# The first layer as another program: shared experts first, 1024 tokens at a time with seven block products, then all typed experts in a row

## The chip, the cores and the metric

The kernel runs on one core of a Trainium2 chip. The metric is the device time of one execution in microseconds; a kernel is timed in several runs and the median is given. TensorE (PE) does the matmuls, and its weight loads are listed apart as PEld. VectorE (DVE), ScalarE (ACT) and GpSimd (POOL) do the elementwise work, and SyncE (SP) issues most of the transfers. Every engine works through its own instructions in order; between engines there are only semaphores.

## What is computed

Four layers, each added to or applied on `x` of 8 x 256 tokens x 256 features, all in fp32. The change touches the first, L0:

```python
def _dense(x, wi, wo):                      # wi 256 x 1024, wo 1024 x 256
    return jax.nn.relu(x @ wi) @ wo
s0, s1, s2 = (_dense(h, share_wi[j], share_wo[j]) for j in range(3))
idx_a, idx_b = type_idx, type_idx + 1       # one type per batch row of 256 tokens
out_a = relu(h @ expert_wi[idx_a]) @ expert_wo[idx_a]
out_b = relu(h @ expert_wi[idx_b]) @ expert_wo[idx_b]
expert_out = out_a * wa + out_b * wb        # wa, wb from softmax(gate_vecs / 0.1)
gi = concatenate([expert_out[:, 0], s0[:, 0], s1[:, 0], s2[:, 0]], axis=-1)
g = softmax(relu(gi @ gate_w1) @ gate_w2)   # four gates per batch row, from its first token
out = expert_out * g0 + s0 * g1 + s1 * g2 + s2 * g3
```

`x = x + L0(x)` is followed by L1 (eight gated experts and a shared one of the same size), L2 (a small adapter with a layer norm) and L3 (a linear map chosen per batch row). These stay as they are.

## The kernel before

Features lie on the 128 partitions in two halves (`DT` = 2), tokens along the free dimension. Each fp32 product is made of three matmuls on a rounded high part and a remainder (`product`: high x high, high x low, low x high, L424 to L426), so weights, inputs and hidden tiles all exist as `hi` (an ACT copy or relu) and `lo` (a subtraction on DVE or POOL).

L0 works in `NB` = 4 blocks of 512 tokens. In each block the list `L0_JOBS` is run: shared expert 0, typed 0, shared 1, typed 1, shared 2, typed 2, typed 3. A job has eight steps, one per 128 hidden features. A step is an up product (`l0_up`, six matmuls into one of four PSUM banks), the relu on ACT (L907), the low part on DVE (L1599), and two steps later the down product (`l0_down`, six matmuls into `sum0` or `sum1`). A shared step works on 512 columns, a typed step on the 256 tokens of a batch row. The twelve weight matrices of the shared experts are loaded once, split once and kept in SBUF (`W`, 96 KB per partition). Typed weights stream through four `raw` buffers in chunks of 512 KB; ACT makes high parts (L874), POOL the low part of the up weights (L1203), DVE that of the down weights (L1622).

`l0_take` moves a finished sum: shared ones to `acc` (L1490), typed ones scaled into `x`. The gate's hidden sum is collected on DVE (`gate_partial`, L1518) and summed over the partitions by small fp32 matmuls (`gate_first`, L513) in step 3 of the next block; `gate_hidden`, `gate_shifted` and `gate_probs` follow in steps 3 to 5, and `mix` adds the parts of the block before to `x` in steps 5, 6 and 16 to 22. The gate of the last block is done in the first steps of L1. Blocks 1 and 2 are one hardware loop.

L1 already uses another scheme. It takes two 512-token blocks and two 128-row weight tiles at a time and replaces eight block products by seven (`block_product`, L552). For that POOL adds and subtracts blocks of `x` (`x_sums`) and of the weights (`weight_sums`), and the results are put together from PSUM banks `A` and `Bk` by ACT copies (L1017) and DVE adds (L1658). Only up products are made so. TensorE's order is written out:

```python
earlier(0); first_products(0); first_products(1); earlier(1)    # earlier(d): down product of the slot before
second_products(0); second_products(1); earlier(2)
third_products(0); third_products(1); earlier(3)
fourth_product(0); fourth_product(1)
```

The weights of L1's first expert are prepared on POOL and ACT in the last L0 block, beside typed and shared steps.

Of the kernel before, what the change touches and what calls it, by code (L numbers as in the profile page):

```python
# [17 lines left out]
B, S, D, F = 8, 256, 256, 1024  # L18
P = 128
# [9 lines left out]
L0_JOBS = [("shared", 0), ("expert", 0), ("shared", 1), ("expert", 1), ("shared", 2), ("expert", 2), ("expert", 3)]  # L29
NJ = len(L0_JOBS)  # L30
L0_STEPS = NJ * FT
L0_ALL = NB * L0_STEPS
EX_STEPS = 4 * FT
EX_CH = EX_STEPS // 2
SUMS = [0, 1, 0, 1, 0, 1, 0]
PLAIN0 = 4 + 4 * NSH
# [28 lines left out]
def job_of_expert(j):  # L65
    return [i for i, (kind, n) in enumerate(L0_JOBS) if kind == "expert" and n == j][0]


def exout_at(k, first, last_block):

    q = (k + 1) // 2
    if k == 0 or (k % 2 == 1) != (q % 4 == 0):
        return None

    if first and q == 5 or last_block and q in (9, EX_CH):
        return None
    return q


def local_step(k):  # L80

    return FT * job_of_expert(k // FT) + k % FT

def stream_table():
    sh = lambda j, m, h: ("plain", 1 + 4 * j + 2 * h + m)
    t = [("plain", 0), sh(0, 0, 0), sh(0, 1, 0), sh(0, 0, 1), sh(0, 1, 1),
         sh(1, 0, 0), sh(1, 1, 0), sh(1, 0, 1), ("expert", 0), ("expert", 1), ("expert", 2), ("expert", 3), ("expert", 4), ("expert", 5),
         sh(1, 1, 1)] + [sh(2, m, h) for h in range(2) for m in range(2)]  # L90
    t += [("plain", 13), ("plain", 14), ("plain", 15)]
    t += [("expert", q) for q in range(6, 58)]
    t += [("plain", PLAIN0 + r) for r in range(3)]
    t += [("expert", q) for q in range(58, 64)]
    t += [("plain", PLAIN0 + r) for r in range(3, L1_CH * NE1 + B)]
    return t
# [6 lines left out]
def build(nc, xT_d, sh_d, ex_d, l1_d, types_d, types_row_d, gvec_d, gw1_d, gw2_d, prob_d, sgate_d, w1_d, w2_d, b1_d, cols_d, w3_d, bias_d, ident_d, out_d):  # L103
# [45 lines left out]
    gpart = place("gate_partial", [P, 2, D], f32)  # L149
# [19 lines left out]
    cg = place("gate_tile", [P, 3, BLK], f32, over="weights", skip=88 * K1)  # L169
    hi = place("hidden_hi", [P, 4, BLK], f32r, over="hidden")  # L170
# [29 lines left out]
    with ctx:  # L200
# [13 lines left out]
        first_hi, first_lo = sem("first_hi"), sem("first_lo")  # L214
        const_full, gw1_full = sem("const_full"), sem("gw1_full")
# [45 lines left out]
        def gate_ps(tb):  # L261

            return sums[0 if isinstance(tb, int) and tb == NB else 1]
# [42 lines left out]
        def raw_fill(key):  # L306

            return 16 * (AT[key] // RAW + 1)
# [1666 lines left out]
```

## Time and profile before

| | |
|---|---|
| median of 3 runs | 1604.03 us (1602.68 to 1605.13) |
| the profiled execution | 1604.2 us, span 1602.4 us |
| instructions | 22577 |
| TensorE busy | 1592.0 us (99%), 7986 matmuls |
| weight loads busy | 1354.9 us (85%) |
| DVE, ACT, POOL busy | 1096.3 (68%), 864.8 (54%), 510.3 (32%) |
| moved by DMA | 79.05 MB, mean 49 GB/s |

Busy shares tell which engine to look at. Matmuls are pipelined, so that the listed duration of one (0.39 us for 512 columns) is longer than the distance between two starts; the distance is what counts. The list of instructions in order of time gives the start, the duration and, in brackets, how long the engine sat idle before it and what ended that. A list of one line's instructions gives the shortest, median and longest duration in ns. A table of stretches gives each engine's busy time in it, TensorE's granted clock as a share of full speed, and the transfers.

### The profile page before, as it was taken

To read this page: it belongs to the slowest core of one execution; us is meant where nothing else is said; L and a number is where in the kernel's file an instruction comes from. 1 tells how busy PE (TensorE), PEld (TensorE's weight loads), DVE (VectorE), ACT (ScalarE), POOL (GpSimd) and SP (SyncE) were. 2 spreads that over 40 slices of the span, in tenths; PEclk is the share of its full clock that TensorE was granted. 3 is DMA by queue.
4 is the path that set the end of the run, shared out by engine and by line. 5 is a ranking of instruction groups with operands and counts; after the bars stand their busy time and mean duration, and the time that the engine had idled before them with its cause. 6 is when DMAs were issued, how large, how long until landed. Compare 5 with 4: busy or idle time off the path is not lost.

```text
span 1602.4 us, 22577 instructions
## 1 busy us (share of the span) xinstructions
PE 1592.0 (99%) x7986; PEld 1354.9 (85%) x7986; DVE 1096.3 (68%) x1661; ACT 864.8 (54%) x1563; POOL 510.3 (32%) x452
## 2 busy tenths in 40 slices
PE   9999999999999999999999999999999999999998
PEld 8898898898897888888888888888888888888888
DVE  6665565466679777777777777776776776656555
ACT  5543343343565665665565565565565565555343
POOL 2121121124745431431431431431431441146110
PEclk9999999999999999999999999999999999999999
DMA  6522131131321010010010010010010000021000
GB/s 226 183 92 68 53 106 52 52 105 53 105 80 40 14 40 27 14 40 27 14 40 27 14 39 27 17 37 27 21 33 27 25 29 27 27 65 44 13 14 27
DMA packets 28763, 79.05 MB, mean 49 GB/s; under 512 B 4838, under 2 KB 9830, under 8 KB 28534
## 3 DMA queue, kind: packets, MB, share of 16 engines
q1 hardware_dynamic: 28070, 76.39, 14.8%
q8 instruction: 58, 0.95, 0.2%
q0 software_dynamic: 304, 1.10, 0.2%
q14 instruction: 43, 0.35, 0.1%
q10 hardware_dynamic: 288, 0.26, 0.1%
HBM read 75.64 MB, written 2.10 MB: 49 GB/s over the span
## 4 chain that ended last, share of the span: by engine, by line
PE 98%; DVE 1%; DMA 0%; issue 0%; ACT 0%; SPq 0%; DVEq 0%
PE sum L424 13%; PE sum L425 13%; PE sum L426 13%; PE up L556 13%; PE up L558 13%; PE up L557 13%; PE up L424 7%; PE up L425 6%; PE up L426 6%; DMA raw<-in_shared 0%; PE sum L738 0%; PE sum L513 0%; PE sum L704 0%; PE sum L764 0%; PE sum L763 0%
## 5 line engine op out<-in xcount | busy, mean ns | idle before, releaser
L1028 ACT ACTIVATE hidden_hi<-up_tile 128x512 fp32r<-128x512 f32 x256 | 161.2, 630 | 187.3 <-DVE up_tile L1663 163.3
L907 ACT ACTIVATE hidden<-up 128x256 fp32r<-128x256 f32 (+1 forms) x224 | 106.3, 475 | 247.0 <-PE sum L426 203.7
L1658 DVE TENSOR_TENSOR gate_tile<-up,gate_tile 128x512 f32<-128x512 f32 x192 | 130.0, 687 | 142.3 <-PE up L558 142.3
L1668 DVE TENSOR_TENSOR hidden_lo<-up_tile,hidden_hi 128x512 fp32r<-128x512 f32 x256 | 196.0, 785 | 44.0 <-ACT hidden_hi L1028 44.0
L1599 DVE SCALAR_TENSOR_TENSOR hidden<-up,hidden 128x256 fp32r<-128x256 f32 (+1 forms) x224 | 120.3, 537 | 154.4 <-ACT hidden L907 153.1
L556 PE MATMUL up<-x_sums,gate_up 128*128 128x512 f32 x512 | 199.5, 390 | 0.0
L426 PE MATMUL sum<-hidden_hi,down 128*128 128x512 f32 x512 | 199.4, 390 | 0.0
L424 PE MATMUL sum<-hidden_hi,down 128*128 128x512 f32 x512 | 199.4, 390 | 0.0
L425 PE MATMUL sum<-hidden_lo,down 128*128 128x512 f32 x512 | 199.4, 389 | 0.0
L558 PE MATMUL up<-x_sums,gate_up 128*128 128x512 f32 x512 | 199.4, 389 | 0.0
L557 PE MATMUL up<-x_sums,gate_up 128*128 128x512 f32 x512 | 199.4, 389 | 0.0
L1663 DVE TENSOR_TENSOR up_tile<-up_tile,gate_tile 128x512 f32<-128x512 f32 x192 | 183.2, 980 | 2.2
L1203 POOL TENSOR_TENSOR expert_in<-raw,expert_in 128x512 fp32r<-128x512 f32 x64 | 83.2, 1300 | 318.1 <-ACT expert_in L874 318.1
L1021 ACT ACTIVATE gate_tile<-gate_tile 128x512 f32<-128x512 f32 x192 | 119.8, 633 | 90.4 <-DVE gate_tile L1658 88.2
L556 PE MATMUL up<-x_hi,gate_up 128*128 128x512 f32 x384 | 149.9, 390 | 0.8 <-DVE up_tile L1663 0.8
L557 PE MATMUL up<-x_lo,gate_up 128*128 128x512 f32 x384 | 149.6, 390 | 0.0
L558 PE MATMUL up<-x_hi,gate_up 128*128 128x512 f32 x384 | 149.6, 390 | 0.0
L1017 ACT ACTIVATE gate_tile<-up 128x512 f32<-128x512 f32 x192 | 110.5, 594 | 72.0 <-PE up L558 65.6
L1203 POOL TENSOR_TENSOR gate_up<-raw,gate_up 128x384 fp32r<-128x384 f32 x64 | 72.3, 1130 | 204.3 <-ACT gate_up L971 204.3
L1658 DVE TENSOR_TENSOR up_tile<-up,up_tile 128x512 f32<-128x512 f32 x192 | 130.2, 687 | 1.9
L1017 ACT ACTIVATE up_tile<-up 128x512 f32<-128x512 f32 x192 | 112.0, 600 | 21.2 <-PE up L558 15.6
L424 PEld LDWEIGHTS sum<-hidden_hi,down 128*128 128x128 f32 x512 | 96.1, 188 | 20.7 <-DVE hidden_lo L1668 0.9
(267 smaller groups left out, 3700.6 us busy)
## 6 DMA issues: line engine op xcount, KB each, us to landing
raw<-in_experts SPq DMA_DIRECT2D x64, 512.0 KB, 3.6
raw<-in_l SPq DMA_DIRECT2D x54, 512.0 KB, 3.5
raw<-in_shared SPq DMA_DIRECT2D x11, 512.0 KB, 5.0
raw<-in_w SPq DMA_DIRECT2D x8, 256.0 KB, 2.5
raw<-in_xT SPq DMA_DIRECT2D x3, 512.0 KB, 5.7
out<-out_stage SPq DMA_DIRECT2D x6, 256.0 KB, 2.1
gate_w<-in_gw POOLq DMA_DIRECT2D x1, 1024.0 KB, 7.8
raw<-in_w SPq DMA_DIRECT2D x16, 64.0 KB, 2.4
```

What stands on the lines that cost most here:

```text
L424: pe.matmul(out, wh, vh, start=start, stop=False)
L425: pe.matmul(out, wh, vl, start=False, stop=False)
L426: return pe.matmul(out, wl, vh, start=False, stop=stop)
L556: pe.matmul(out, wh, vh, start=first, stop=False, skip_group_check=True)
L557: pe.matmul(out, wh, vl, start=False, stop=False, skip_group_check=True)
L558: return pe.matmul(out, wl, vh, start=False, stop=True, skip_group_check=True)
L1017: A(out, ps, ACT.Copy).then_inc(q_done[m], 1)
L1028: A(hi[:, i], cu[:, i], ACT.Copy).then_inc(hi_done, 1)
L1203: return nc.gpsimd.tensor_tensor(dst, src, hi.bitcast(f32), ALU.subtract)
L1658: V.tensor_tensor(t, ps, t, ALU.add).then_inc(c_done[m], 1)
L1663: V.tensor_tensor(cu[:, i], up, cg[:, RING[i]], ALU.mult).then_inc(gat_done, 1)
L1668: V.tensor_tensor(lo[:, i], cu[:, i], hi[:, i].bitcast(f32), ALU.subtract).then_inc(lo_done, 1)
```

## The change

L0 becomes two programs in a row.

**Shared experts.** 24 slots: two halves of 1024 tokens, three experts, four weight pairs. A slot makes the up products of one pair for 1024 tokens with seven block products (`shared_up`, 21 matmuls of 512 columns) and the down products of the slot before (`shared_down`, 4 x 6). Slot 0 makes its four tiles directly, with 24 matmuls, as long as no sums exist. Weights are no longer kept: 24 chunks stream in for the first half and again for the second, and are summed and split each time. ACT copies the first contributions out of PSUM, DVE adds, ACT makes relu and high part, DVE the low part. `x` is now loaded straight into its tile. The shared sums of all four blocks are stored in separate places (`accs`).

**Typed experts.** Four blocks of 32 steps of 256 columns, written out, with no loop. The gate's shared part is made once for all batch rows on TensorE (`gate_shared`); `gate_partial` goes. Mixing is split: `mix_start` on DVE in steps 5 and 6, the scaling of two shared sums on ACT in steps 7 to 10, six additions on POOL (`x_add`), the last shared sum on DVE in steps 20 and 21 (`mix_end`). The preparation of L1's first weights is spread over typed blocks 0 and 1 from three chunks staged apart (`stage`), and that of its x sums over block 3. The last block is mixed in L1 as before.

```diff
-L0_JOBS = [("shared", 0), ("expert", 0), ("shared", 1), ("expert", 1), ("shared", 2), ("expert", 2), ("expert", 3)]
+NJ = 4
+NA = 2 * NSH * 4
 ...
+            sp.dma_start(x[:, 0, 0:BLK], xT_d[:, 0, 0:BLK]).then_inc(first_x, 16)
+            sp.dma_start(x[:, 1, 0:BLK], xT_d[:, 1, 0:BLK]).then_inc(x_in[0], 16)
+            load_x(1)
+            sp.dma_start(raw[:, 0, FIRST[2]], sh_d[0][:, FIRST[2]]).then_inc(raw_full[0], 16)
+            load_chunk(("first", 0), sh_d[1])
 ...
+                    load_chunk(("expert", EX_CH * tb + q), ex_d[t[q // 4] * 4 + q % 4])
+                    if tb == 0 and q == 1:
+                        sp.wait_ge(sh_b[1], 3 * 12)
+                        for r in range(STAGED):
+                            sp.dma_start(stage[:, r], l1_d[r]).then_inc(stage_full[r], 16)
 ...
 TensorE:
+            def shared_slot(a):
+                if a == 0:
+                    shared_first_tiles()
+                    return
+                shared_up(a, "first")          # waits for the low parts of its weight pair (w_lo)
+                shared_down(a - 1, 0)
+                if a > 1:
+                    shared_up(a - 1, "fourth")
+                shared_down(a - 1, 1)
+                shared_up(a, "second")         # waits for x sums 1 to 3, ACT's first copy, DVE's first add
+                shared_down(a - 1, 2)
+                shared_down(a - 1, 3)
+                shared_up(a, "third")
 ...
+                    if tb and n == 3:
+                        if tb == 1:
+                            gate_shared()
                         gate_first(tb)
 ...
 ACT, from slot 0's last tiles on:
+            for i in range(2):
+                shared_x_hi(0, i)
+            act.wait_ge(sh_sum, 4)
+            A(agu[0][:, 0, 1, 3 * P:7 * P], aws[0][:, 1, 3 * P:7 * P], ACT.Copy).then_inc(w_hi, 1)
+            for i in range(2, 4):
+                shared_x_hi(0, i)
+            first_part(adn[1][:, 0].rearrange("p f n -> p (f n)"), raw[:, 1, 512:1024])
 ...
 ACT, at the end of shared_slot(a), behind sh_copied(a, 2), sh_copied(a, 1):
+                if a == 1:
+                    shared_up_hi(1)
+                    shared_down_hi(1)
+                elif a % 2 == 0 and a + 2 < NA:
+                    shared_up_hi(a // 2 + 1)
+                elif a % 2 == 1 and a + 1 < NA:
+                    shared_down_hi((a + 1) // 2)
+                if a in (2, 3):
+                    x_in_hi(a)
 ...
 POOL:
+            shared_x_sum(0, 0)
+            shared_x_sum(0, 1)
+            shared_sums(0)
+            shared_x_sum(0, 2)
+            shared_up_lo(0)
+            shared_x_sum(0, 3)
+            for p in range(1, NAP):
+                shared_sums(p)
+                shared_up_lo(p)
+                shared_down_lo(p)
+                if p == 1:
+                    for i in range(4):
+                        shared_x_sum(1, i)
+                if p in (3, 4):
+                    for i in range(2):
+                        shared_x_lo(1, 2 * (p - 3) + i)
 ...
+            for q in range(NB * EX_CH):
+                expert_lo(q)
+                if q in AFTER:                 # early_sum, early_up_lo, early_down_lo, x_add, x_sum, ...
+                    AFTER[q]()
 ...
 DVE, shared_slot(a): adds and low tiles, then
+                if a in (2, 3):
+                    x_in_lo(a)
+                if a % 4 == 0 and a < NA:
+                    gr, j, _ = shared_of(a - 1)
+                    shared_take(gr, j, 0)
+                    shared_take(gr, j, 1)
 ...
 DVE, l0_block(tb), step n:
+                    if tb and n in (5, 6):
+                        mix_start(tb, n - 5)
+                    if tb and n in (20, 21):
+                        mix_end(tb, n - 20)
 ...
 ACT, l0_block(tb), step n:
+                    if tb and 7 <= n <= 10:
+                        scaled_shared(tb, (n - 7) // 2, (n - 7) % 2)   # waits for both mix_start
```

## Rows read from the trace of the kernel before

**Rows 1.** The page: busy time per engine, and the chain that ended last by engine.

```profile
PE 1592.0 (99%) x7986; PEld 1354.9 (85%) x7986; DVE 1096.3 (68%) x1661; ACT 864.8 (54%) x1563; POOL 510.3 (32%) x452
...
PE 98%; DVE 1%; DMA 0%; issue 0%; ACT 0%; SPq 0%; DVEq 0%
```

**Rows 2.** List in order of time, TensorE, shared steps: start, duration, instruction.

```profile
194.62 0.39 PE L424 MATMUL sum<-hidden,weights 128*128 128x512 f32 x1
...
205.96 0.39 PE L426 MATMUL sum<-hidden,weights 128*128 128x512 f32 x1
```

**Rows 3.** List in order of time, TensorE, typed steps in a row.

```profile
447.00 0.28 PE L424 MATMUL up<-x_hi,expert_in 128*128 128x256 f32 x1
...
449.76 0.28 PE L426 MATMUL sum<-hidden,expert_out 128*128 128x256 f32 x1
```

**Rows 4.** List in order of time at the start; then a piece of the chain there.

```profile
6.83 0.63 ACT L942 ACTIVATE weights<-raw 128x512 fp32r<-128x512 f32 x1 [0.23 <-DMA raw<-in_shared]
...
12.43 0.40 PE L424 MATMUL up<-x_hi,weights 128*128 128x512 f32 x1
...
2.13 6.35 DMA raw<-in_shared
```

**Rows 5.** List in order of time, POOL (380 to 497) and ACT (420): preparing L1.

```profile
380.40 1.75 POOL L1236 TENSOR_TENSOR x_sum_tiles<-x 128x512 f32<-128x512 f32 x1
...
386.44 5.94 POOL L1203 TENSOR_TENSOR x_sums<-x_sum_tiles,x_sums 128x512 fp32r<-128x512 f32 x4
...
419.51 0.79 POOL L1262 TENSOR_TENSOR weight_sums<-raw 128x256 f32<-128x256 f32 x1
...
422.93 1.02 POOL L1203 TENSOR_TENSOR gate_up<-raw,gate_up 128x384 fp32r<-128x384 f32 x1
...
475.30 1.01 POOL L1203 TENSOR_TENSOR gate_up<-raw,gate_up 128x384 fp32r<-128x384 f32 x1
...
480.20 1.02 POOL L1203 TENSOR_TENSOR gate_up<-raw,gate_up 128x384 fp32r<-128x384 f32 x1
...
496.85 2.56 POOL L1203 TENSOR_TENSOR down<-raw,down 128x512 fp32r<-128x512 f32 x2 [11.23 <-ACT down L980]
...
420.30 0.84 ACT L970 ACTIVATE gate_up<-raw 128x768 fp32r<-128x768 f32 x1
421.04 1.05 ACT L971 ACTIVATE gate_up<-weight_sums 128x1024 fp32r<-128x1024 f32 x1
```

**Rows 6.** One line's instructions, DVE: shortest, median and longest ns; SBUF inputs, then PSUM.

```profile
L1663 DVE TENSOR_TENSOR up_tile<-up_tile,gate_tile x192: 676/693/1786, 462.5 to 1411.9; 128x512 f32<-128x512 f32 x192
L1663 DVE TENSOR_TENSOR up_tile<-up,gate_tile x64: 676/691/692, 469.7 to 1413.4; 128x512 f32<-128x512 f32 x64
```

**Rows 7.** TensorE near the end; a stretch (length, busy per engine, granted clock, DMA).

```profile
1571.04 0.30 PE L424 MATMUL up<-x_hi,l_w 128*64 128x256 f32 x1 [2.39 <-DVE x_lo L1788]
1572.06 0.41 PE L425 MATMUL up<-x_lo,last_gate_up 128*128 128x256 f32 x1
1572.27 0.41 PE L426 MATMUL up<-x_hi,last_gate_up 128*128 128x256 f32 x1
...
1572.00:1574.00 2.00, 2.00 (x12) 2.00 (x11) 0.84 (x2) 0.85 (x3) 0.00 (x0) 0.50 0.00 0
```

**Rows 8.** Stretch of typed steps in a row: length, PE, PEld, DVE, ACT, POOL busy, clock.

```profile
433.00:457.50 24.50, 24.50 (x193) 23.90 (x192) 19.35 (x31) 12.63 (x29) 14.32 (x13) 1.00 0.46 151
```

**Rows 9.** The gate's small matmuls in the chain; two blocks, one looped, one unrolled.

```profile
127.49 0.79 PE sum L513 x8
...
127.20:240.47 113.27, 113.27 (x684) 101.27 (x683) 64.76 (x115) 43.95 (x90) 23.25 (x17) 1.00 0.24 75
...
353.70:466.60 112.90, 112.90 (x684) 101.27 (x683) 75.16 (x118) 54.38 (x106) 57.68 (x49) 1.00 0.26 85
```

**Rows 10.** POOL's queue: its configuration records and its first tensor instruction.

```profile
L1203 POOLq MODIFY_POOL_CONFIG  x2: 37/37/37, 9.0 to 9.1; - x2
...
24.79 1.28 POOL L1203 TENSOR_TENSOR expert_in<-raw,expert_in 128x512 fp32r<-128x512 f32 x1 [15.77 <-ACT expert_in L874]
```

More of the change, by code:

```diff
@@ L62, with gu_at, dn_at @@
 STAGES += ["split", "beta", "scaled", "base", "final"]
[L65 to L82, printed above, removed]
-def stream_table():
[L87 to L96, printed above, removed]
+def gu_at(p):
+    return max(2 * p - 1, 0)
+def dn_at(p):
+    return 2 * p
+def stream_table():
+    t = [("plain", 0), ("first", 0)] + [("plain", o) for o in range(1, PLAIN0)]
+    t += [("expert", q) for q in range(NB * EX_CH)]
+    return t + [("plain", PLAIN0 + r) for r in range(STAGED, L1_CH * NE1 + B)]
 STREAM = stream_table()
@@ L261, in gate_ps @@
         def gate_ps(tb):
-            return sums[0 if isinstance(tb, int) and tb == NB else 1]
+            return sums[0]
         def ex_slot(n):
@@ new lines, in shared_down @@
+            def shared_down(a, d):
+                g, j, s = shared_of(a)
+                f, to = TILES[d]
+                pe.wait_ge(sh_lo[d], a + 1)
+                if a < 2:
+                    pe.wait_ge(first_lo, 8 + a)
+                elif a % 2 == 0:
+                    pe.wait_ge(w_lo, dn_at(a // 2) + 1)
+                if s == 0 and d < 2 and a:
+                    pe.wait_ge(sh_taken, 2 * (3 * g + j) - 1 + to)
+                for m in range(DT):
+                    c = slice(m * P, (m + 1) * P)
+                    last = product(sums[1 - to][:, m, :], adn[a % 4][:, 0, f, c], adn[a % 4][:, 1, f, c], hi[:, d], alo[:, d],
+                                   s == 0 and d < 2, s == 3 and d >= 2)
+                last.then_inc(sh_down[d], 1)
@@ L481, in l0_down @@
                 if f == 0:
-                    before = [i for i in range(jj) if SUMS[i] == SUMS[jj]]
-                    if before:
-                        pe.wait_ge(sum_taken, NJ * tb + before[-1] + 1)
-                    elif not first:
-                        back = [i for i in range(NJ) if SUMS[i] == SUMS[jj]][-1]
-                        pe.wait_ge(sum_taken, NJ * tb - NJ + back + 1)
-                    if jj == 1 and not first:
-                        pe.wait_ge(gate_shift, tb)
-                c = slice(0, BLK) if job[0] == "shared" else ex_slot(n)
@@ L812, in scaled_part @@
                     last.then_inc(scaled_done, 1)
-            l0_block(0, first=True)
-            with pe.Fori(1, NB - 1) as tb:
+            for a in range(NA):
+                shared_slot(a)
+            for tb in range(NB):
                 l0_block(tb)
-            l0_block(NB - 1)
             for e in range(NS):
```

1016 lines of the change are left out of this document (635 added, 381 removed).

## The prediction

> **What bounds the kernel now.** I read the page first: TensorE is busy 99% of the span at full clock, and 98% of the chain that ended last is TensorE [rows 1]. A busy share does not say how dense the stream is, so the next view is the instruction list: a matmul over 512 columns starts every 0.2267 us (51 starts from 194.62 to 205.96, [rows 2]), one over 256 columns every 0.120 us (24 starts from 447.00 to 449.76, [rows 3]), and inside layer 0 hardly anything interrupts them. So the kernel costs its matmuls, plus what it loses at the start, at the gates and at the end. All other engines have room on average (DVE 68%, ACT 54%, POOL 32%); what counts is where one of them is late for a matmul. The sum is made against the profiled execution, 1604.2 us, 0.2 above the median of 1604.03.
>
> **Matmuls removed.** Shared experts before: 4 blocks x 24 steps x 12 = 1152 matmuls of 512 columns. After: 24 slots x (21 up + 24 down) = 1080, and 3 more, because slot 0 makes its four tiles directly (24 instead of 21): 1083. Only the up half of a shared expert becomes cheaper, 7/8 of it. 69 x 0.2267 = **-15.6 us**. The typed experts keep their 1536 matmuls of 256 columns. L1 keeps its own.
>
> **Small things on TensorE.** The gate's share of the shared experts moves from DVE to TensorE: 12 small fp32 matmuls, once. Four such take 0.79 us before [rows 9]; **+2.4**. The four per block remain. The loop over blocks is written out: the unrolled block is 112.90 us against 113.27 of a looped one [rows 9], so 2 x 0.35; with DVE's gate_partial gone from the front of L1 (a 0.8 us wait is near it, I give it 0.4), **-1.1**.
>
> **The start.** This is the disputed term, since the new program needs much more preparation before its second pair of slots. Before, TensorE's 25th matmul of the work starts at 12.43 [rows 4]: 24 x 0.2267 = 5.4, so 7.0 us lie outside the work. After, I follow the queues.
>
> - x block 1 (512 KB) now comes ahead of the last 256 KB weight part. Before, that part is used at 6.83, and the 512 KB chunk after it has landed at 8.48 [rows 4], 1.65 us for 512 KB; so block 1 lands at about 7.7, and tiles 2 and 3 of slot 0 start at 9.7 (two ACT copies, DVE's low parts). TensorE then has slot 1's first products and half of slot 0's down products, to 16.5.
> - POOL makes everything slot 1 still lacks, in one queue: two x sums (4 take 6.04, [rows 5]), four half-size weight sums (2.2, half the size of those that take 3.42), a third x sum, a low part (1.3), the fourth x sum: 18.2. ACT stands in its queue at the copy of that fourth sum, and only behind it (and one down copy) makes slot 1's first copy, which the second products wait for: **20.1**, TensorE idle 3.6 us.
> - Slot 2's first products need pair 1's low parts. POOL: sums 3.4 to 21.5; ACT is not free before 23 to 23.5 (its three copies of slot 1) and splits pair 1 (0.84 and 1.05, [rows 5]); POOL's four low parts take 4.90 [rows 5]: **30.4**. TensorE has been out of work since 26 to 27.4.
> - Then POOL: down low parts 2.5, four x sums of the second half 6.0 to 6.8, sums of pair 2 3.4: 42.6. ACT waits for them in slot 2's queue (pair 2), and behind them copies x block 2 (1.05); DVE waits for this copy (x_in_lo, 1.2) at the end of slot 2, ahead of slot 3's first add. So slot 2's fourth product, which TensorE could start at 43.4 to 45, starts at **47 to 48**, and the down product behind it at about 50.
> - At that point 126 matmuls are done, 28.6 us of work: 21.5 us outside the work against 7.0. The start costs **+14.5**. POOL's serial work alone, with never a wait for ACT, gives 8.5 (lower bound); with every DVE instruction held and three clock drops it is 17.
>
> The half clock is in this: before, after an idle TensorE of 2.39 us the granted clock is 0.50 (the 1.2 GHz level) for at least 2 us, in which 256-column matmuls come every 0.21 us [rows 7]; each such drop costs 1 to 1.6 us of work, partly hidden in the next wait. The Trainium skill (TensorE: Matmul & The Clock Gate, "Why this matters for your kernels") likewise advises against idle gaps between bursts; by that rule the change pays beyond its three gaps, and the trace agrees with 2.39 us idle and 0.50 granted.
>
> From slot 4 on the pipeline holds. A slot is 45 x 0.2267 = 10.2 us. DVE has seven instructions of 0.7 (3 adds, 4 low tiles), ACT seven of 0.6 and 1.9 of weights, POOL 11 to 12 us per pair of slots, 20.4. Each tile is ready 0.7 to 2 us before its down product even if DVE is held once: a DVE instruction with both inputs in SBUF takes 0.69 us alone and up to 1.79 beside POOL, one that reads PSUM 0.69 always [rows 6]. The two takes (1.2 each) end just as the next slot's adds are due. I cost the steady slots at nothing; without this cover it would be some 0.5 us per slot.
>
> **From shared to typed.** SP issues the three staged L1 chunks (1.5 MB) ahead of expert chunks 2 and 3, so chunk 2 lands near 8 us into the first typed slot, when it is due; DVE takes two sums and makes the first low parts between them. **+1.5** (0 to 3).
>
> **All typed experts in a row.** A typed step is 12 x 0.120 = 1.44 us. From 433 to 457.5, where typed steps run in a row already, TensorE is busy all 24.5 us and ACT 12.6 of them [rows 8]. New is that the gate and the mixing of a block now lie in typed steps 3 to 10, not in shared steps of 2.72. DVE in steps 5 and 6: three small ones, two mix_start (0.75), a low part of weights (0.69) and two hidden tiles (0.42) are 3.2 against 2.88, more if held; ACT's scaling waits for both mix_start ahead of its next relu. I follow it step by step to a wait of 0.9 us per block (0.5 without holding, 2.3 with all of it), three blocks: **+2.7** (1.5 to 7). POOL has 1.30 per two steps plus one added instruction (1.3 to 1.75) against 2.88, on 35 of the 64 chunks: on the edge, costed at nothing.
>
> One page bears on POOL's first instruction. In the trace of before, POOL's configuration records stand at 9.0 us, and the first tensor instruction only waits for ACT much later, so nothing shows a loading time [rows 10]. The Trainium skill (GPSIMD Engine Reference, "2.1 Instruction dispatch") says that the first call to a freshly loaded kernel pays a load of about 6 us that no instruction shows. By that, POOL's first x sum would start near 10 and not 7.7, and as ACT has slack there the start would cost about 1.3 us more, an estimate from this page; the trace does not decide, and the sum does not use it.
>
> **Sum.** -15.6 + 2.4 - 1.1 + 14.5 + 1.5 + 2.7 = +4.4; 1604.2 + 4.4 - 0.2 = **1608.5 us** (forecast, chance 0.42, its own range 1605 to 1613).
>
> **Rivals.**
> 1. The start costs only POOL's serial work, and neither the crossing nor the typed blocks wait: -15.6 + 2.4 - 1.1 + 8.5 = -5.8, **1598.2 us**, faster. The point that decides: ACT free at the moment the pair 1 sums are ready, and slot 2's fourth product by 43.5. For it: waits I add can overlap. Against it: ACT's queue order. Chance 0.18.
> 2. The start as worked out, but the typed run has no wait: -15.6 + 2.4 - 1.1 + 14.5 = +0.2, **1604.2 us**, no change. For it: at 433 to 457.5 DVE worked 19.35 of 24.5 us and TensorE never waited. Chance 0.22.
> 3. POOL does not keep up with the typed run: 1.30 + 1.75 held is 3.05, with a delay by DVE on both 3.2, against 2.88, so 0.2 to 0.3 late on each of 35 chunks once its lead of about 1.2 us is used: some 8 us more than the forecast, **1617 us**. For it: POOL's durations in the trace reach 1.75; against it: most are 1.30. Chance 0.18.
>
> **Numbers.** Range 1598 to 1617. A measurement of this kernel can tell about 0.2% (3.2 us) from no change: below 1600.8 is faster, above 1607.2 slower. Faster: most of rival 1 and a tail of rival 2, 0.20. Same: most of rival 2 and the lower part of the forecast, 0.29. Slower: the rest of the forecast and rival 3, 0.51.
>
> **What would show it.** In the profile after: 69 fewer 512-column matmuls at the same 0.227 us spacing; TensorE idle near 17 to 20, 26 to 30 and 44 to 47, each ended by ACT copies or POOL low parts, with granted clock 0.5 behind them; the first typed matmul at about 261 us; small waits on DVE and ACT in steps 5 to 9 of typed blocks 1 to 3; L1's first product some 4.5 us later than before. I am wrong if the stalls of the first 50 us sum to under 12 us, if the steady slots are longer than 10.3 us, or if typed blocks are longer than 32 x 1.44 = 46.1 us plus 2 to 3 us.

## The result and the profile after

The changed kernel takes **1621.78 us** (median of 4, 1620.72 to 1623.1) against 1604.58 for the kernel before in the same comparison (4 runs, 1602.68 to 1605.26): ratio **1.0107** (95%: 1.0095 to 1.0119), 17.2 us slower. The forecast of 1608.5 us has the right sign; the size is wrong, and the time lies above the range of 1598 to 1617. All times of stretches below are from the profiled execution, 1622.5 us with a span of 1620.7.

The page after, first busy times, then the granted clock in 40 slices and the chain that ended last by engine; they answer to [rows 1]:

```profile
PE 1591.2 (98%) x7941; PEld 1351.8 (83%) x7941; DVE 1132.7 (70%) x1661; ACT 938.3 (58%) x1696; POOL 682.8 (42%) x600
...
PEclk8999999999999999999999999999999999999999
...
PE 93%; DVE 3%; ACT 1%; POOL 1%; issue 1%; DMA 0%; SPq 0%; ACTq 0%; DVEq 0%
```

TensorE is as busy as before, though it has 15.6 us less to do: at half clock matmuls of 512 columns start every 0.43 us instead of every 0.2267, and all of that time counts as busy. What tells is the chain, from 98% TensorE to 93%, and the view of waits (what TensorE waited for, us in total, times, longest):

```profile
PE sum L438 <- DVE expert_out L2004: 5.2, 7, 1.7
PE up L438 <- DVE x_lo L1840: 4.1, 1, 4.1
PE up L446 <- POOL shared_up L1429: 3.3, 1, 3.3
PE up L446 <- ACT gate_tile L998: 3.1, 1, 3.1
...
PE sum L625 <- DVE gate_products L1950: 1.9, 1, 1.9
...
PE sum L438 <- DVE shared_lo L1845: 1.1, 1, 1.1
```

Two groups: four waits of the first 55 us (x_lo, shared_up, gate_tile, shared_lo), and the low parts of the typed down weights (`expert_out`) with the gate, all behind 265 us. The sums of waits are smaller than the loss, so I kept books by time: from a mark to a mark, less the matmuls between at 0.2267 and 0.120 us.

| stretch | time | work | outside the work | in the kernel before | loss |
|---|---|---|---|---|---|
| to the first typed matmul | 265.5 | 239.4 (1056 matmuls) | 26.1 | 7.0 (to 12.43) | +19.1 |
| from there to L1's first product | 211.2 | 189.0 | 22.2 | 6.1 | +16.1 |
| work of L0 | | | | | -15.6 |
| L1's first product to the end | 1144.0 | | | 1145.3 | -1.3 |

The sum is 18.3 us, the two profiled executions differ by 18.3. The forecast had +14.5 for the first row and, gates, crossing, mixing and loop together, +5.5 for the second: the start is 4.6 us over it, the typed run 10.6. The steady slots are as forecast: from 55 to 270 us TensorE is busy 215.0 of 215 us.

**The start.** The chain, then the list in order of time (brackets: idle before, and what ended it):

```profile
1.70 8.08 DMA x<-in_xT
...
10.47 2.95 DVE x_lo L1840 x2
```

```profile
13.46 0.80 PE L438 MATMUL up<-x_hi,shared_up 128*128 128x512 f32 x1 [4.14 <-DVE x_lo L1840]
...
18.99 0.60 ACT L1003 ACTIVATE hidden_hi<-up 128x512 fp32r<-128x512 f32 x1 [1.96 <-PE up L440]
...
21.22 1.44 POOL L1429 TENSOR_TENSOR shared_up<-shared_sums_up,shared_up 128x512 fp32r<-128x512 f32 x1 [4.70 <-ACT shared_up L1076]
...
26.14 0.77 PE L446 MATMUL up<-shared_x_sums,shared_up 128*128 128x512 f32 x1 [3.05 <-ACT gate_tile L998]
...
36.57 0.77 PE L446 MATMUL up<-x_hi,shared_up 128*128 128x512 f32 x1 [3.26 <-POOL shared_up L1429]
...
54.60 0.50 PE L438 MATMUL sum<-hidden_hi,shared_down 128*128 128x512 f32 x1 [1.09 <-DVE shared_lo L1845]
```

The four gaps are those of the forecast (9.7, 20.1, 30.4, about 50), 3.8 to 6.2 us later. The lines to look at are the second and the third: POOL, which I took to work without a pause, stands 4.70 us waiting for ACT's copy of the weight sums, and ACT stands ahead of it at slot 0's last tile, which TensorE had only just made.

**The typed run.** One line's instructions (shortest, median, longest ns), the low parts of the typed down weights, in the kernel before and in the changed one:

```profile
L1622 DVE TENSOR_TENSOR expert_out<-raw,expert_out x64: 678/693/1373, 25.3 to 456.1; 128x512 fp32r<-128x512 f32 x64
```

```profile
L2004 DVE TENSOR_TENSOR expert_out<-raw,expert_out x64: 674/1204/1848, 273.4 to 475.6; 128x512 fp32r<-128x512 f32 x64
```

Two stretches of the changed kernel (length, busy of PE, PEld, DVE, ACT, POOL, granted clock, DMA), around the gate of block 1:

```profile
323.00:328.00 5.00, 5.00 (x39) 5.00 (x37) 1.73 (x3) 0.90 (x2) 1.94 (x2) 0.80 0.52 185
328.00:333.00 5.00, 5.00 (x25) 5.00 (x25) 2.40 (x10) 1.34 (x4) 0.00 (x0) 0.51 0.09 19
```

And the list in order of time at the gate of the last block:

```profile
429.80 1.29 POOL L1429 TENSOR_TENSOR expert_in<-raw,expert_in 128x512 fp32r<-128x512 f32 x1
431.05 1.26 POOL L1429 TENSOR_TENSOR x_sums<-x_sum_tiles,x_sums 128x512 fp32r<-128x512 f32 x1
...
429.90 2.43 DVE L1947 TENSOR_SCALAR gate_products<-gate_w,gate_hidden 128x4 f32<-128x4 f32 x2
...
432.78 0.39 PE L625 MATMUL sum<-gate_products,ones 128*128 128x8 f32 x2 [1.93 <-DVE gate_products L1950]
```

The median low part takes 1.20 us where it took 0.69, since POOL now works beside typed steps far more. The 12 small matmuls of the shared gate (from 323.64) and the block's own gate take 4.5 us. The clock falls during them, near 326, without an idle gap ahead of it, and half clock lasts for another 4.6 us behind them. And two instructions of four columns take 1.21 and 1.31 us, 2.43 together, beside two POOL instructions of 1.3.

By block, from the first typed matmul over the three gates (326.4, 378.3, 428.4) to L1: 60.9, 51.8, 50.1 and 48.4 us, of which outside the products 4.4 (2.8 of it the shared gate), 5.8, 4.0 and 8.0. A block's own gate, two sets of small matmuls, is about 1.2 of each of the last three.

### The profile page after: what moved, and what is told of

The parts are those of the page before. It is cut to its first block, busy times and chain, and to the rows that moved or that the text cites. A ratio compares the mean times of both kernels' runs of the same rounds, so it can differ in the third digit from the quotient of the medians.

```text
span 1620.7 us, 22419 instructions
## 1 busy us (share of the span) xinstructions
PE 1591.2 (98%) x7941; PEld 1351.8 (83%) x7941; DVE 1132.7 (70%) x1661; ACT 938.3 (58%) x1696; POOL 682.8 (42%) x600
## 4 chain that ended last, share of the span: by engine, by line
PE 93%; DVE 3%; ACT 1%; POOL 1%; issue 1%; DMA 0%; SPq 0%; ACTq 0%; DVEq 0%
PE up L670 13%; PE up L672 12%; PE up L671 12%; PE sum L438 12%; PE sum L440 12%; PE sum L439 12%; PE up L438 4%; PE up L439 3%; PE up L440 3%; PE up L446 2%; PE up L448 2%; PE up L447 2%; DVE expert_out L2004 1%; DMA x<-in_xT 0%; DVE x L1987 0%
## 5 line engine op out<-in xcount | busy, mean ns | idle before, releaser
L1429 POOL TENSOR_TENSOR gate_up<-raw,gate_up 128x384 fp32r<-128x384 f32 x60 | 68.0, 1133 | 204.2 <-ACT gate_up L1198 204.2
L1243 ACT ACTIVATE up_tile<-up 128x512 f32<-128x512 f32 x192 | 112.1, 600 | 21.3 <-PE up L672 15.6
L1556 POOL TENSOR_TENSOR weight_sums<-raw 128x256 f32<-128x256 f32 x30 | 28.9, 963 | 204.7 <-PE up L672 204.7
L670 PEld LDWEIGHTS up<-x_sums,gate_up 128*128 128x128 f32 x512 | 96.1, 188 | 20.2 <-ACT gate_tile L1243 0.2
## 6 DMA issues: line engine op xcount, KB each, us to landing
x<-in_xT SPq DMA_DIRECT2D x3, 512.0 KB, 10.2
```

Source lines behind the costliest of these rows:

```text
L670: pe.matmul(out, wh, vh, start=first, stop=False, skip_group_check=True)
L1243: A(out, ps, ACT.Copy).then_inc(q_done[m], 1)
L1429: return nc.gpsimd.tensor_tensor(dst, src, hi.bitcast(f32), ALU.subtract)
```

## The experiments

Every profile is read at the same marks: first typed matmul, the gates of blocks 2 and 3, L1's first product, the span (us).

| kernel | first typed | gate 2 | gate 3 | L1 | span | outside the work to first typed |
|---|---|---|---|---|---|---|
| before | | | | 457.08 | 1602.4 | |
| changed | 265.54 | 378.25 | 428.36 | 476.72 | 1620.7 | 26.1 |
| s1_order | 261.06 | 374.21 | 424.32 | 472.65 | 1616.4 | 21.7 |
| s2_loads | 263.86 | 376.83 | 426.95 | 475.33 | 1619.2 | 24.5 |
| s3_queue | 261.00 | 373.76 | 423.89 | 471.47 | 1616.9 | 21.6 |
| t1_gate | 266.58 | 378.06 | 428.17 | 475.78 | 1621.2 | 27.2 |
| t2_adds | 263.33 | 376.77 | 425.57 | 473.71 | 1619.1 | 23.9 |
| t3_lows | 263.25 | 377.68 | 427.81 | 474.56 | 1618.5 | 23.9 |
| d1_direct | 255.15 | 366.62 | 416.75 | 465.94 | 1609.9 | 15.1 |
| d2_direct_gate | 255.62 | 366.75 | 416.86 | 463.60 | 1609.0 | 15.5 |
| d3_start | 250.97 | 361.93 | 412.06 | 460.41 | 1604.5 | 10.9 |
| d4_all | 249.78 | 361.72 | 410.59 | 457.60 | 1603.0 | 9.7 |
| d5_all | 249.56 | 363.54 | 412.42 | 457.72 | 1603.1 | 9.5 |
| d6_all | 250.32 | 362.32 | 411.22 | 456.50 | 1600.3 | 10.2 |

(From d1_direct on there are 1059 matmuls up to the first typed one, 240.1 us.) When x block 1 has landed shows in POOL's first instruction, which waits for nothing else. The changed kernel and t1 to t3 have the same start and give 263.3 to 266.6, with that landing at 8.4 to 9.9: a first typed matmul is good to 3 us from one profile. From POOL's first instruction to the first typed matmul these four take 254.8 to 257.0 us, s1_order 252.0, s2_loads 255.8, s3_queue 251.4; this takes the landing out of the comparison. From gate 2 to gate 3 all nine profiles with the original mixing there give 50.11 to 50.13.

### s1_order: the queue of ACT at the start

```diff
-tiles 1, 3 of slot 0; x sums 0, 1; weight sums of slot 1; x sums 2, 3      # ACT; DVE's low parts alike
+x sums 0, 1; weight sums of slot 1; tile 1; x sum 2; tile 3; x sum 3
```

> Against the changed kernel; ScalarE (ACT) copies the x sums 0 and 1 and slot 1's weight sums ahead of slot 0's tiles 1 and 3, DVE's low parts follow the same order. Theory A, order of ACT's queue: in the changed kernel POOL stands from 16.5 to 21.2 us waiting for ACT's copy of the weight sums, which stands behind the copy of slot 0's last tile (TensorE, 19.0). Then POOL's low part moves from 21.2 to about 16.5, slot 1's second products from 26.1 to about 21, slot 2's first products from 36.6 to 31 to 32, the first typed matmul from 265.5 to 260 to 261: 4.5 to 5.5 us less. Theory B, the preparation as such is too long (POOL's serial work and the half clock behind each gap): what the first gap gives back is lost in the next, first typed matmul at 264 or later, under 1.5 us less.

First typed matmul at 261.06, 4.5 us earlier, kernel 1618.3 us (one run). POOL's low part no longer waits:

```profile
14.50 0.63 ACT L1073 ACTIVATE shared_up<-shared_sums_up 128x512 fp32r<-128x512 f32 x1 [1.44 <-POOL shared_sums_up L1468]
...
15.66 1.73 POOL L1428 TENSOR_TENSOR shared_up<-shared_sums_up,shared_up 128x512 fp32r<-128x512 f32 x1
...
23.83 0.50 PE L446 MATMUL up<-shared_x_sums,shared_up 128*128 128x512 f32 x1 [0.56 <-DVE gate_tile L1848]
```

Theory A, though slot 1's second products start at 23.8 and not at the expected 21. About 1 us of the 4.5 is x block 1, which landed earlier here (copied at 8.96); counted from POOL's first instruction, 2.8 to 5.0 us are won. It is an order, not an amount of work, that made POOL late.

### s2_loads: the loads behind x block 1

```diff
+            sp.wait_ge(x_in[1], 16)
             load_chunk(("first", 0), sh_d[1])      # and all later loads
```

> Against the changed kernel; the loads behind the first weight parts (a down chunk, two weight chunks, x blocks 2 and 3) are issued only once x block 1 has landed. Theory A, the transfers share the engines: x block 1 lands at 7.7 to 8.3 instead of 9.8, tiles 2 and 3 of slot 0 start at 11.5 to 12 instead of 13.5, and the first typed matmul is 1.5 to 2 us earlier (if slot 1's weight chunk, now landing later, is not what is late next; then 0). Theory B, x block 1 waits only for the bytes issued before it: it lands at 9.8 again, and the kernel is 0 to 2 us slower, since down chunk and pair 1 land some 4 us later.

ACT's copy of x block 1 starts at 7.96 instead of 9.81, TensorE's tiles at 11.63 instead of 13.46, the first typed matmul 1.7 us earlier; kernel 1621.1 us (one run). The time alone shows nothing: t2_adds and t3_lows, whose start is that of the changed kernel, reach the first typed matmul at 263.3, earlier than the 263.86 here. The landing does: in the three profiles in which the chunks wait for x block 1 (this, d5_all, d6_all) POOL's first instruction starts at 8.07 to 8.09, in the ten others at 8.4 to 9.9. So transfers issued later can delay it; my 7.7 for the landing had counted only the bytes ahead. The gap behind x block 1 is not its landing alone, though: DVE's two low parts, 1.3 us in the forecast, took 2.95 beside POOL's sums.

### s3_queue: x blocks 2 and 3, and the second half's x sums

```diff
+                if a in (2, 3): x_in_hi(a)          # ACT: ahead of shared_up_hi, shared_down_hi
-                if p == 1: 4 x shared_x_sum(1, i)   # POOL
+                if p == 2: 4 x shared_x_sum(1, i)
```

> Against the changed kernel; ACT copies x blocks 2 and 3 ahead of the weights of pairs 2 and 3, and POOL makes the four x sums of the second half behind pair 2's low parts instead of ahead of pair 2's sums. Theory A: DVE's low part of x block 2 (50.65 us) is what slot 2's fourth product waits for, so it moves to about 46, the half clock and the 1.1 us wait at 54.6 go, and the first typed matmul is 3 to 4 us earlier. Theory B: the wait only moves to slot 4's first products (pair 2's low parts) or to slot 3's tiles, under 1 us is won.

First typed matmul 4.5 us earlier (3.4 to 5.6 counted from POOL's first instruction), kernel 1618.8 us (one run). The fourth product's wait is gone. Part of it comes back, as theory B said, once:

```profile
70.46 0.50 PE L438 MATMUL sum<-hidden_hi,shared_down 128*128 128x512 f32 x1 [1.66 <-DVE shared_lo L1845]
```

### t1_gate: the small matmuls one by one

```diff
-                        if tb == 1: gate_shared()        # 12 fp32 matmuls in a row, step 3
+                    if spread[0]: gate_shared()          # one behind every third matmul, steps 3 to 5
```

> Against the changed kernel; the 12 small fp32 matmuls of the gate's shared part stand one by one behind every third matmul of typed steps 3 to 5 of block 1 instead of in a row, the block's own gate follows two steps later. Theory A: in a row they cost 2.9 us plus a drop of the granted clock to half (328 to 333 us, about 2.4 us); spread, the drop goes: no half clock there, block 1 about 2 to 2.5 us shorter. Theory B: the drop comes from something else, or small matmuls between others cost more each (their weight load is not hidden): block 1 equally long or longer by up to 3 us.

The half clock is gone (1.00 granted from 320 to 370 us, 0.93 in the changed kernel), but from the first typed matmul to gate 2 only 1.2 us are won (111.5 against 112.7), not 2 to 2.5. d1_direct shows why. There the 12 matmuls stand in a row as in the changed kernel, yet no half clock followed; instead the waits appear which the slow matmuls had covered, 0.23, 0.26, 0.33 and 0.75 us from 324 to 332, and the same stretch takes 111.5 us too. So the half clock costs 1.2 us net against this profile of the changed kernel, and spreading the matmuls wins nothing over an execution without it: the slow stretch gave DVE time. The 1.2 is not a fixed price: other executions with the drop take 112.8 to 114.4, but d3_start, with its 12 matmuls in a row and 0.50 granted from 313.7 to 317.1, takes only 111.0.

### t2_adds: POOL's additions of the mixing

```diff
-G(x[:, dt, sl], x[:, dt, sl], other, ALU.add)
+G(x[:, dt, sl][:, 0:1], x[:, dt, sl][:, 0:1], other[:, 0:1], ALU.add)
```

> Against the changed kernel; POOL's 18 additions of the mixing (three typed blocks, six each) work on one column instead of 512, so the mixed x is wrong. Theory A, in the typed run DVE's low parts with both inputs in SBUF are held by POOL's instructions and so come late for the down products: without the additions the waits at steps 10 to 20 of blocks 1 to 3 go (343.7, 349.7, 394.1, 400, 446.8, 452.7, 458.8 us), first typed matmul to L1's first product 2 to 3 us shorter. Theory B, DVE's own number of instructions makes them late: under 0.5 us.

The kernel leaves out 511 of the 512 columns of each addition.

```profile
L2004 DVE TENSOR_TENSOR expert_out<-raw,expert_out x64: 673/694/1781, 271.2 to 472.6; 128x512 fp32r<-128x512 f32 x64
```

The median low part falls from 1.20 to 0.69 us without a change on DVE. From gate 2 to gate 3 it takes 48.80 instead of 50.11: 1.3 us, and the wait of 0.75 in step 12 is gone. Two waits of 0.28 and 0.33 us in steps 8 and 9 stay. Over the whole typed run 0.8 us are won, not the 2 to 3 expected: the stretch to gate 2 was 0.7 longer here, the last block only 0.2 shorter. But in this execution the last block has a drop of the clock (0.51 granted from 430.5 to 434) that the changed kernel's profile has not, so its time is no clean reading. TensorE's waits in blocks 1 to 3 fall from 7.1 to 4.8 us. Theory A in the mechanism; the size in time is shown by block 2 alone, 1.3 us.

### t3_lows: L1's x sums in the last block

```diff
-for i, at in enumerate((3, 4, 11, 12)):      # chunk of the last block behind which POOL makes low part i
+11: low part 0; 12: low part 1; 13: low parts 2 and 3
```

> Against the changed kernel; in the last typed block POOL makes the first two low parts of L1's x sums behind chunks 11 and 12 instead of 3 and 4 (the other two behind 13). Theory A: DVE's gate products (four instructions of 4 columns), of which the first two took 2.43 us beside POOL instead of 0.36 in block 1, are held by these low parts, and the wait of 1.93 us at 432.8 goes, as does part of the 1.7 at 440: 2 to 3 us less. Theory B: they are late for another reason (ACT, the sums' take), nothing changes; or the low parts, now close to the end of the block, are late for L1 and give 1 us back.

The gate products' wait falls from 1.93 to 0.84 us, that of 1.68 at 440 us to 0.34; gate 3 to L1's first product takes 46.8 instead of 48.4. 1.6 us, under the expected 2 to 3. The stretch to gate 2, which the edit doesn't touch, was 1.7 longer in this execution, so that the typed run as a whole shows nothing (211.3): only the local reading decides. The first of the two gate products still takes 1.21 us, beside POOL's expert low part, which was not moved; the second, beside which the moved low part had stood, falls from 1.31 to 0.22. So instructions of four columns were held by POOL.

### d1_direct and d2_direct_gate: slot 1 without sums

```diff
+T0(0) T0(2) T1(0) T1(2)                      # TensorE: tiles of slots 0 and 1, first 512 tokens
+T0(1) down(0,0) T0(3) down(0,2) T1(1) down(0,1) T1(3) down(0,3) down(1,0) down(1,2) up(2,"first")
-shared_sums(0); shared_up_lo(0)              # POOL
```

> Against the changed kernel; slot 1 is made directly as slot 0 (24 matmuls instead of 21, no sums of x or of its weights needed), TensorE makes its two tiles of the first 512 tokens while x block 1 is under way, POOL goes straight to the x sums and pair 1; later loads wait for x block 1, and ACT copies x blocks 2 and 3 ahead of weights. Theory A, the start is lost to preparation that pair 0 needs: with 27 matmuls' worth of tiles more in hand, TensorE waits only for x block 1 (about 14 us, 24 matmuls done), slot 2 follows at about 30, pair 1 being ready at 25 to 27; first typed matmul at 249.5 to 252, so 14 to 16 us less, kernel 1606 to 1608. Theory B, POOL's preparation (x sums 6.2, pair 1 8.6 plus ACT's copies, pair 2) is what limits the first 50 us in any order: slot 2 or slot 4 waits, first typed matmul at 257 or later, 1612 or more.

> The start of the run before, the spread gate of block 1 and the moved low parts of block 3 together. If the three are independent: 15 + 2 + 2.5 us less than the changed kernel, 1602 to 1604, that is equal to the kernel before. If the start only moves the preparation's lateness on: 1608 or more.

The diff shows a part: loads behind the down chunk also wait for x block 1, slot 0's last weight part is issued ahead of it, ACT copies x blocks 2 and 3 ahead of weights as in s3_queue, and the tiles of both slots have new places in the queues of ACT and DVE.

d1_direct: 1611.7 us (one run), first typed matmul at 255.15, so 15.1 us outside the work instead of 26.1, for three matmuls more. How much of the 11.0 us comes from making slot 1 directly was not separated: no run has the changed orders of s1_order, s2_loads and s3_queue together without it, and s1_order and s3_queue alone won 4.5 each. x block 1 leaves 1.0 us of idle time, slot 2's first products start at 27.44 with 0.35. That fits theory A, but is 3 to 6 us short of its number, and one wait accounts for most of them:

```profile
39.18 0.84 ACT L1047 ACTIVATE shared_up<-raw 128x768 fp32r<-128x768 f32 x1 [5.79 <-POOL shared_sums_up L1511]
...
42.64 0.79 PE L439 MATMUL sum<-hidden_hi,shared_down 128*128 128x512 f32 x1 [3.91 <-DVE shared_lo L1883]
```

ACT stands 5.79 us at a copy for slot 4, and slot 2's tile, which TensorE needs now, is behind it. d2_direct_gate: 1610.76 us (5 runs), 1.0039 (1.0025 to 1.0053) of the kernel before, outside its expected 1602 to 1604, with the same stall; the typed run won 2.8 us (208.0 against 210.8).

### d3_start and d4_all: that stall, and the rest of the typed run

```diff
-p == 1: x sums of the second half            # POOL, ahead of pair 2's sums
+p == 2, ahead of shared_down_lo(2)
-a == 2: constants()                          # DVE; now a == 5
-mix_start in steps 5, 6                      # d4_all alone: 5, 7 (ACT's scaling 8 to 11)
```

> Slot 1 made directly, as before; in addition POOL makes the four x sums of the second half behind pair 2's first low parts (not ahead of pair 2's sums), and DVE's constants and ACT's exponentials of the type gates stand two to three slots later. Theory A, what is left of the start in d1_direct is one stall: ACT stood 5.8 us at the copy of pair 2's sums (39.2 us), with slot 2's tile behind it in its queue, TensorE idle 3.9 us at 42.6 and at half clock after it. Then pair 2's sums are ready at 33.5, the stall goes, and the first typed matmul moves from 255.2 to 249 to 250.5; kernel 1605.5 to 1607. Theory B, POOL's total work up to slot 4 is the limit and the stall comes back elsewhere (slot 4's first products, the low parts of the second half's sums, the take behind slot 4, as at 70.5 us in s3_queue): 253 or later.

> The same start; the spread gate, the moved low parts of the last block, and mix_start in steps 5 and 7 instead of 5 and 6 (ACT's scaling one step later). Block 2 of the typed run, from gate to gate, has taken 50.11 us in every run but the one without POOL's additions (48.80). Theory A, DVE's pile-up in steps 5 to 8 costs the two small waits (0.28 and 0.33 us) there: block 2 takes 49.3 to 49.6; first typed matmul to L1's first product 206 to 207.5 (211.2 in the changed kernel); kernel 1602 to 1604, just faster than the kernel before or equal. Theory B, the waits of a block are those of its additions and takes alone: block 2 stays at 50.1, kernel 1604 or more.

d3_start: 1607.38 us (10 runs), ratio 1.0018 (1.0008 to 1.0027). First typed matmul at 250.97, 4.2 us earlier, 0.5 later than theory A's bound, and the kernel 0.4 above its 1607. The stall is gone, and nothing came back but 0.41 us at 60.4. The constants and exponentials moved in the same run; that the order of POOL's sums is the cause rests on the wait, which ended with those sums. It would be some 1.5 us more with the same first 10 us: here the first matmuls ran at half clock (every 0.43 us until 9.8), ACT stood at slot 0's tiles and copied x block 1, landed at 9.5, only at 11.2; in d1_direct it did so at 9.6. Of the start's loss of 19.1 us against the kernel before, 3.9 are left (10.9 against 7.0), and 0.7 of work for three matmuls.

d4_all: 1606.11 us (11 runs), 1.0008 (0.9999 to 1.0017). From gate 2 to gate 3 48.87 us instead of 50.11 to 50.13: theory A, with more than the expected 0.5 to 0.8, as much as t2_adds won by leaving the additions out: either end of the pile-up can be relieved. The typed run takes 207.8 us (expected 206 to 207.5), and the kernel's time is 2 us above the expected; the list shows two waits for POOL, the larger in block 1 (2.3), this one in the last block:

```profile
451.78 0.36 PE L439 MATMUL up<-x_hi,expert_in 128*128 128x256 f32 x1 [1.28 <-POOL expert_in L1482]
```

### d5_all and d6_all

```diff
 d5: the down chunk too waits for x block 1; x sum low part 3 behind chunk 15; mix_end in steps 19, 21
 d6: block 1 alone: additions from chunk 6 (not 5), mix_start in 7, 8, mix_end in 22, 23
```

> As d4_all, and: the down chunk too is loaded only once x block 1 has landed (it landed at 9.6 and 11.2 us in the last two profiles, and the kernel's own runs spread by 4 us); of L1's x sum low parts in the last block two no longer stand behind one chunk of POOL (there TensorE waited 1.28 us for POOL's expert low part at 451.8); mix_end stands in steps 19 and 21 instead of 20 and 21 (waits of 0.28 and 0.69 us at 443 and 445). Theory A, each of these waits is a matter of what stands together in a queue: x block 1 lands at 8.0 to 8.8 in every run, first typed matmul at 248.5 to 249.5, last block (gate to L1's first product) 45 to 45.6 instead of 47.0; kernel 1602.5 to 1604.5 with a spread under 2.5 us. Theory B, the engines' load in these steps is full and the waits only move: last block 46.5 or more, kernel 1605.5 to 1606.5 again.

> As d5_all, with the queue order of block 1 alone changed: its mixing starts two steps later than in the other blocks (its gate does), so POOL's additions now begin one chunk later (they stood waiting for DVE 3.5 us, with the expert low part behind them for which TensorE waited 2.3 us at 326.9), and DVE's mix_end stands in steps 22 and 23 instead of 19 and 21 (there DVE waited for POOL's last addition and TensorE 1.55 us at 343.8). Theory A: both waits go, block 1 (gate to gate) takes 47.2 to 48 instead of 49.65, L1's first product 455.5 to 456.5 in a profile with the same start, kernel 1602 to 1604, faster than the kernel before by 0.05 to 0.2%. Theory B, POOL with 1.30 and 1.75 us per chunk is itself at TensorE's pace of 2.9 us in these steps, so the waits only come later: block 1 at 49 or more, kernel 1605.

d5_all: 1605.05 us (11 runs), 1.0000 (0.9991 to 1.0009), spread 2.7 us (d4_all 4.0); expected were 1602.5 to 1604.5 and under 2.5. Both local parts of theory A are there: x block 1 landed at 8.1 (in d6_all too; 9.2 to 9.7 in d1 to d4), and the last block takes 45.3 us. But ACT copies x block 1 only at 9.8, behind slot 0's second tile, so the start wins nothing; and time came back in block 1, 49.65 us instead of 48.08 between its gate and gate 2:

```profile
326.91 0.36 PE L439 MATMUL up<-x_hi,expert_in 128*128 128x256 f32 x1 [2.30 <-POOL expert_in L1482]
343.79 0.36 PE L439 MATMUL sum<-hidden,expert_out 128*128 128x256 f32 x1 [1.55 <-DVE expert_out L2063]
```

d6_all mends these two by order alone: block 1 takes 47.90, L1's first product is at 456.50, and the kernel takes **1602.39 us** (11 runs, 1600.77 to 1603.57) against 1605.13 (15 runs): 0.9986 (0.9977 to 0.9995). It is the only version faster than both kernels, by 0.14% against the kernel before, which is less than the 0.2% of the forecast's scale. In its profile block 1 still waits 1.54 us for one low part.

Not all of this gain lies in layer 0. In the profiles d6_all reaches L1's first product 1.2 us before d5_all and 0.6 before the kernel before; the other 1.5 us against either are the stretch behind it, where d5_all and the kernel before have a drop of the clock (0.96 granted from 1560 to 1600) and d6_all has none (1.00). The mean granted clock is 1.000 in 7 of the 11 runs of d6_all and in 1 of the 15 of the kernel before; whether the new order has to do with that is open. In layer 0 the 15.6 us of matmuls saved are all but used up: the start costs 3.2 us more than before and three matmuls 0.7, the typed run 11.1.

## Why the forecast was wrong

**Matmuls, -15.6.** Right, at the same spacing; L1 is untouched.

**gate_shared, +2.4.** 2.8 (323.64 to 326.42). What I had not foreseen is the half clock behind it, 1.2 us net in this profile (t1_gate, d1_direct), in d3_start nothing.

**Start, +14.5.** It cost 19.1. The gaps, their place and their cause were named rightly, their times were 3.8 us late at the first one and 4.6 to 6.2 at the others. The first error is a term: landing at 7.7 (it was 9.8 in the profile, 8.0 with the chunks behind it held back), and 1.3 us for DVE's two low parts that took 2.95 beside POOL, although [rows 6] gave the held duration, which I had used in the typed run and not here. The second is a step left out: I had POOL work through, and did not put slot 0's tiles 1 and 3 into ACT's queue ahead of the weight sums (s1_order, up to 4.5 us). Nor do POOL's terms up to 18.2 add up: from 7.7 they give 17.2, and the last sum gives 1608.4 us. Half clock was in the sum with 1 to 1.6 us for each of three drops; about 32 matmuls came every 0.43 us or more (12, 6 and 14 behind the three gaps), some 6.5 us gross. How much of that another wait would have cost was not measured. The upper bound of 17 assumed every hold and three drops and was still too low, since it took the landing for certain.

**Steady slots, 0.** Right.

**Crossing, +1.5.** A wait of 0.27 us and a few slow starts, about 1 us in all. Right.

**Typed blocks' mixing, +2.7.** This is the step that failed most. Beyond the gates the changed kernel loses 1.6 us in block 0 (the crossing is in it), about 1 in block 1 (the half clock covers the rest), 2.7 in block 2 and 6.8 in the last. With the gates, the crossing and the half clock taken out of the +16.1, 9 to 11 us are left for this term (an estimate from the books). The prediction's own sign of being wrong is met: blocks 1 and 2 take 51.8 and 50.1 us, over 46.1 plus 2 to 3. I had followed DVE's queue with 0.69 us for the low part and held values as an extra; the held value is the rule there (median 1.20). And I had looked at the mixing alone: the last block also carries the x sums for L1, which in the kernel before lay beside shared steps of twice the length, and these met the gate's small instructions (1.9 and 1.7 us, t3_lows). The last block alone all but reaches the bound of 7 for three.

**Loop and gate_partial, -1.1.** Not taken apart by any run.

**The rivals.** Rival 1 (start costs POOL's serial work) is refuted by ACT's queue, but d3_start shows that its kind of number can be had with slot 1 made directly and other orders: 10.9 us outside the work, 3.9 more than before where this rival had 8.5. Rival 2, a typed run without a wait, rested on the stretch of 24.5 us in [rows 8]; that stretch has no gate and no mixing in it. Rival 3 gave 1617 us and was nearest, by the wrong mechanism: in the changed kernel's profile no typed step waited for POOL itself; it made DVE late. POOL's own lateness exists: in block 0, which these runs share with the changed kernel, TensorE waited 0.25 to 0.77 us for it in s3_queue, t1_gate, t2_adds and t3_lows, and up to 2.3 us later on (d4_all, d5_all), where it had stood waiting for DVE or had two extra instructions behind one chunk.

**The page on POOL's first instruction.** The traces decide most of it now. In s2_loads POOL's configuration records stand at 4.2 us and its first tensor instruction starts at 8.07, 0.11 behind ACT's copy of the same x block: 3.9 us, and those were spent waiting for the transfer. The Trainium skill (GPSIMD Engine Reference, "2.1 Instruction dispatch") gives about 6 us for such a load; one that began at 4.2 would have ended at 10.2, and no such time is seen here. A load of under 3.9 us could be hidden in the wait.

## What to carry to other kernels

Saved matmuls pay only when what prepares them has room, and at the start of this kernel it had none. Doing the second unit plainly too (three more matmuls, 0.7 us), together with other orders of loads and of ACT's queue, bought 11 us; how much of that the orders alone would buy was not measured, so try them first. To forecast such a start, write down each engine's queue in full, and ask of each instruction that waits what is queued behind it; a copy for slot 4 ahead of a tile for slot 2 cost 4 us, and order alone took the typed run from 211.2 to 206.2 us. What the new layout costs there stays: 17.2 us outside the work in d6_all against 6.1 before. When elementwise work is moved from long steps to short ones, take the durations held by the other engine as the normal case.

## What the hardware showed

**DVE and POOL.** Instructions of DVE that read only SBUF are held for the length of POOL's: 0.69 us becomes 1.20 in the median and 1.85 at most, and a TENSOR_SCALAR of four columns took 1.2 us instead of 0.23. The relu with one input in PSUM took 404 to 427 ns in all 128 cases. The Trainium skill (SBUF — State Buffer, "SBUF: two separate sides") describes the pair of ports that the two share as an exclusive lock, which goes to whichever starts first and for its whole instruction. The traces agree: the short instructions of DVE ran about as long as POOL's beside them (1.21 and 1.31 us beside 1.29 and 1.26). I had read [rows 6] as a matter of large tiles.

**The granted clock** of the changed kernel fell to half in the course of small fp32 matmuls (in s3_queue and d3_start 0.5 and 1.2 us behind them), during which TensorE is listed as busy throughout (5.00 of 5.00 us, 323 to 328), with no idle gap; a clock that only idle time brings down, which I had assumed, is not what this trace shows. It fell in seven of the eight profiles with the 12 in a row (not in d1_direct) and in none of the five with them spread. Behind the small matmuls it stayed down for 4.6 us in the changed kernel and in t3_lows, 3.4 in s3_queue. What a drop costs differs: the last block of the changed kernel's order takes 48.3 to 48.4 us in four profiles without one, 47.6 in s3_queue and t1_gate and 49.2 in d1_direct with one, since the slow matmuls cover waits.

**Transfers.** The 512 KB of x block 1, issued at 1.70 us, landed between 8.4 and 9.9 with the same program (by POOL's first instruction), and at 8.0 with the chunks behind them held back (s2_loads). Even that is 6.3 us, while the median of the typed chunks of the same size is 3.3; the transfers issued ahead of it are the likely reason, which no run tested.

**The end.** From L1's first product to the end, profiles with the same instructions fall into two groups: 1143.8 to 1144.1 us in seven without a drop of the clock there, 1145.3 to 1145.5 in seven with one, so that this drop costs 1.4 us. The changed kernel was in the first group and the kernel before, with its half clock near 1572 us, in the second; that explains the -1.3 of the books, which is no gain of the change.
